# Cross attention with routed experts on one Trainium2 core: value products of two steps in one block, and work moved from VectorE to ScalarE

## The reference, cut to what matters

```python
x = x + xattn(layernorm(x), ctx, mask)     # x, ctx: 8 x 256 x 512, mask: 8 x 1 x 512
x = x + ffn(layernorm(x))
# xattn: q, k, v = W @ input + b, 16 heads of 16 rows
dot  = mask * (q^T k) / 4 - (1 - mask) * 1e6          # 512 x 512 for each batch and head
amap = softmax(dot, axis=-1) * mask
out  = einsum('bhts,bhds->bhdt', amap, v)
# ffn: 2048 tokens of 512, 8 experts, the best two of each token
logits = x @ gate^T ; weights of the best two, divided by their sum
out = sum over the two of  w2_e @ (silu(g) * u),  g, u = split(w1_e @ x)   # w1: 704 x 512, w2: 512 x 352
```

## Time and profile before

| | us |
|---|---|
| median of 3 runs | 869.19 (865.51 to 871.01) |
| the profiled execution | 871.53 |
| its span, first to last instruction | 869.7 |
| PE busy in the span | 801.8 (92%) |
| DVE busy | 553.6 (64%) |
| POOL busy | 370.3 (43%) |
| ACT busy | 318.6 (37%) |
| mean granted clock of TensorE | 0.972 |

### The profile page before, as it was taken

One profiled execution on the slowest core, in us unless ns is written; L12 is line 12 of the kernel. 1 busy time (PEld: TensorE's weight loads), 2 busy tenths in 40 slices (PEclk: granted clock), 3 DMA queues, 4 the chain that ended last, 5 costly groups with the idle time before them and its releaser, 6 DMA issues. The chain is left out here.

```text
span 869.7 us, 13002 instructions
## 1 busy us (share of the span) xinstructions
PE 801.8 (92%) x3757; PEld 365.1 (42%) x3758; DVE 553.6 (64%) x1071; ACT 318.6 (37%) x619; POOL 370.3 (43%) x392
## 2 busy tenths in 40 slices
PE   5888898989999998999989988899999999999993
PEld 2322332333333433433333332365555665665661
DVE  5778887889888887888877874445433333333331
ACT  0035465556565565665655666522000000000000
POOL 7544364556565655655745423334211221211221
PEclk9579999999999999999999999999999999999997
DMA  6745577666766866856845542354648546354332
GB/s 188 231 129 145 172 203 221 200 209 210 231 206 184 264 196 182 257 163 177 244 127 160 172 113 83 94 144 110 152 89 227 133 110 172 65 156 72 72 51 34
DMA packets 84524, 138.02 MB, mean 159 GB/s; under 512 B 14765, under 2 KB 40685, under 8 KB 84474
## 3 DMA queue, kind: packets, MB, share of 16 engines
q1 hardware_dynamic: 68970, 108.65, 41.8%
q0 software_dynamic: 7744, 17.86, 10.7%
q10 hardware_dynamic: 7760, 10.89, 4.5%
HBM read 77.36 MB, written 59.36 MB: 157 GB/s over the span
## 5 line engine op out<-in xcount | busy, mean ns | idle before, releaser
L843 ACT ACTIVATE pr<-sc 128x512 f32<-128x512 f32 x512 | 267.1, 603 | 219.5 <-PE sc L1507 219.3
L990 DVE TENSOR_REDUCE mx<-tile 128x2 f32<-128x1024 f32 x256 | 309.0, 1216 | 55.9 <-PE tile L1519 50.3
L1507 PE MATMUL sc<-qk 100*128 100x512 bf16 x512 | 154.8, 384 | 9.9 <-DMA qk<-mxt 7.2
L1519 PE MATMUL tile<-qk 97*128 97x512 bf16 x496 | 150.9, 388 | 14.0 <-DVE mx L990 7.9
L765 POOL DMA_INDIRECT out_dram<-xin,ids x36 | 56.4, 1566 | 224.0 <-DVE ids L1312 220.0
L1545 PE MATMUL pvb<-pr,vp 128*32 128x512 f32 x1024 | 138.0, 611 | 0.0
L1660 PE MATMUL pvb<-wring,qkf 128*128 (+1 forms) x216 | 98.7, 593 | 1.6 <-DVE qkf L1322 1.6
L720 POOL TENSOR_SCALAR parts<-qkf 128x512 bf16<-128x512 f32 x31 | 46.9, 1512 | 123.3 <-DVE qkf L1074 119.3
L1519 PEld LDWEIGHTS tile<-qk 97*128 97x128 bf16 x496 | 35.0, 98 | 145.6 <-issue 75.7
L1639 PE MATMUL tile<-wring,xh 128*128 x288 | 91.3, 460 | 0.0
L1639 PE MATMUL sc<-wring,xh 128*128 x288 | 91.2, 459 | 0.0
(11 more groups left out here) (158 smaller groups left out, 789.1 us busy)
## 6 DMA issues: line engine op xcount, KB each, us to landing
qk<-stack_d SPq DMA_DIRECT2D x32, 768.0 KB
stack_d<-parts SPq DMA_DIRECT2D x32, 384.0 KB, 3.1
wring<-w_dram SPq DMA_DIRECT2D x32, 352.0 KB, 7.2
cin<-routed_d ACTq DMA_DIRECT2D x36, 257.0 KB, 3.6
stack_d<-parts SPq DMA_DIRECT2D x32, 256.0 KB, 3.1
pv_d<-ov SPq DMA_DIRECT2D x32, 256.0 KB, 3.4
xin<-x_dram SPq DMA_DIRECT2D x16, 256.0 KB, 5.4
cin<-ctxt_dram SPq DMA_DIRECT2D x8, 512.0 KB, 6.3
```

The source lines that it names most:

```text
L843: nc.scalar.activation(pr[s % 2][:, j, :], sc[(32 * u + 4 * s + j) % NSC][:, :], ACT.Exp, scale=SCALE).then_inc(exped.sem, 1)
L990: dve.tensor_reduce(cols, t[:, :, :], X, ALU.max, negate=True).then_inc(drained.sem, 1)
L1507: nc.tensor.matmul(sc[(32 * u + 4 * s + j) % NSC][:, :], ks[half(u)][0:ALL_ROWS, h, c * P:c * P + P], qs[half(u)][0:ALL_ROWS, h, :], start ...
L1519: last = nc.tensor.matmul(t[:, i, :], qs[half(w)][0:RAW_ROWS, h, c * P:c * P + P], ks[half(w)][0:RAW_ROWS, h, :], start=True, stop=True)
```

## The change

Five edits, which hang together:

1. PE's order in units 2 to 15 is written out by hand. The products now stand in blocks of two: those of steps 6 and 7 of the unit before in step 0, those of steps 0 and 1 in step 2, 2 and 3 in step 4, 4 and 5 in step 6. Tiles are placed around them; `count_early` in the last unit moves from step 2 to step 4, `transpose_rows(0, 0)` stays at the end of step 5. DVE's `unit` and the list of tiles (`STEADY`) follow. `product(TAIL, 6)` moves behind the last unit.
2. `pr` gets a third buffer (`NPR = 3`). Its space comes from `mall` and `mrow`, which now lie in `ov`.
3. ACT normalizes the inputs from its third unit on (`normalize` in step 1). POOL makes the shift for it, one small instruction more.
4. ACT copies the second token row (`token_twin` in step 3, and twice in the second part) in place of DVE's second `token_normalize`.
5. DVE reads the logits from PSUM, without the copy `lg`. On POOL `token_rstd` comes before `values_out`.

The first two units keep their order (`front`, `front_events`).

```diff
+NPR = 3
+STEADY = (0, 1, 2, "v", 3, 4, 5, 6, "q", "xT", 7, 8, 9, 10, "logits", 11, 12, "maxT", 13, "k", "ranks", 14, 15)
...
-        pr = [sb(f"pr{i}", [P, 4, T]) for i in range(2)]
+        pr = [sb(f"pr{i}", [P, 4, T]) for i in range(NPR)]
...
+                pool.wait_ge(rstd.sem, rstd.at(u, "pow"))
+                pool.tensor_scalar(at[:, 10:11], at[:, 6:7], at[:, 8:9], -1.0, ALU.mult, ALU.mult
+                                   ).then_inc(rstd.sem, 1)
...
+            def token_twin(u):
+                act.wait_ge(normed2.sem, normed2.at(u, "n"))
+                nc.scalar.activation(xa[:, half(u), 1, 0:T], xa[:, half(u), 0, 0:T], ACT.Copy
+                                     ).then_inc(twin.sem, 1)
...
+                act.wait_ge(rstd.sem, rstd.at(u, "shift"))
...
+                nc.scalar.activation(xh[:, parity(w), half(w), :], xin[:, half(w), :], ACT.Identity,
+                                     bias=at[:, 10:11], scale=at[:, 8:9]).then_inc(normed.sem, 1)
...
-                            if j == 0 and (due := pved.at(u, s, back=2)) is not None:
+                            if j == 0 and (due := pved.at(u, s, back=NPR)) is not None:
...
+                    if s == 1 and u > 1:
+                        normalize(u - 1)
+                    if s == 3 and has(u - 2):
+                        token_twin(u)
...
-                if step == 0:
-                    dve.tensor_copy(lg[:, :], tile_of(u, "logits")[:, 0, 0:E]).then_inc(drained.sem, 1)
...
-                    dve.max(v8[:, :], lg[:, :]).then_inc(choice.sem, 1)
+                    dve.max(v8[:, :], tile_of(u, "logits")[:, 0, 0:E]).then_inc(choice.sem, 1)
```

DVE's `unit` now has the two halves of the reciprocals with the query's drain and the input statistics between them:

```diff
+                maximum(u, *pair_of(u, 5))
+                reciprocals(u, 0)
+
+                maximum(u, *pair_of(u, 6))
+                token_normalize(u)
                 if u == TAIL:
                     plan_early()
...
+                projection_out(u, 0)
+                batch_stats(u, 0)
+                batch_stats(u, 1)
                 reciprocals(u, 1)
-                projection_out(u, 0)
```

More of the change, by code:

```diff
@@ L131, in tile_events @@
         max_ = [(n, ("max", *pair)) for pair in pairs_of(n, s)]
-        ev += max_[:1]
-        if s == 7 and has(n - 2):
-            ev.append((n, "ranks"))
-        ev += max_[1:]
-        ev += [(n, name) for name in fillers(n, s)]
+        ev += max_
+        if s == VALUES_AT[n]:
+            ev.append((n, "v"))
+        if s == 3:
+            ev.append((n, "q"))
         if n == 0 and s == 0:
@@ L141, in tile_events @@
         ev += [(n, ("maxT", *part)) for part in maxima_of(n, s)]
-        if s == 7 and has(n + 3):
+        if s == 7:
             ev.append((n, "k"))
-        if n == TAIL and s == 2:
-            ev.append((n, "early"))
-        if n == LAST - 1 and s == 7:
-            ev.append((n, "count"))
+    return ev
+def tile_events(n):
+    if 0 <= n < len(FRONT):
+        return front_events(n)
+    ahead = {"v": 1, "q": 3, "k": 3, "xT": -2, "logits": -2, "ranks": -2, "maxT": 1}
+    ev = []
+    for name in STEADY:
+        if name == "xT" and n == TAIL:
+            ev.append((n, "early"))
+        if name == "maxT":
+            if has(n + 1):
+                ev.append((n, ("maxT", n + 1, ALL)))
+        elif name in ahead:
+            if has(n + ahead[name]):
+                ev.append((n, name))
+        elif has(pair_of(n, name)[0]):
+            ev.append((n, ("max", *pair_of(n, name))))
+    if n == LAST - 1:
+        ev.append((n, "count"))
     return ev
@@ L369, in attention @@
         rstd2 = Count(sem("rstd2"), of(-2, "eps", "pow"))
-        normed2 = Count(sem("normed2"), of(-2, 0, 1))
-        choice = Count(sem("choice"), of(-2, "v8", "i8", "i8f", "sel", "selb"))
+        normed2 = Count(sem("normed2"), of(-2, "n"))
+        twin = Count(sem("twin"), of(-2, "t"))
+        choice = Count(sem("choice"), of(-2, "v8", "i8f", "sel", "selb"))
         gate_exp = Count(sem("gate_exp"), of(-2, "e"))
@@ L1691, in unit @@
                         project(u, 0)
-                        transpose_tokens(u)
-                    if u == TAIL and s == 2:
-                        count_early()
-                    if s == 4:
-                        logits(u)
-                    if u == TAIL and s == 5:
-                        transpose_rows(0, 0)
                     for w, g in maxima_of(u, s):
@@ L1720, in _ @@
             pe.sem_inc(down_done, 1)
-            for u in range(UNITS):
+            for u in range(len(FRONT)):
+                front(u)
+            for u in range(len(FRONT), UNITS):
                 unit(u)
@@ L1745, in _ @@
             off = gate(0, 0)
+            product(TAIL, 6)
             product(TAIL, 7)
```

210 lines of the change are left out of this document (136 added, 74 removed).

## The result

The changed kernel takes 890.38 us (median of 4 runs, 887.23 to 897.46), the kernel before 868.12 (median of 4, 865.51 to 871.01): a ratio of 1.0267, 95% interval 1.019 to 1.0344. The forecast was 869.0, no change, with 856 to 883 as its range. The time lies above that range. One of the four executions of a0 further down, the 901.51 one, ran in the chip's slower state, so a0 is taken by its other three, 882.77 to 895.71 with a median of 891.17.

What follows compares the result with a forecast made beforehand. PE was taken to bound the kernel, busy 386.7 of 411.5 us in units 2 to 14. The terms -8.6 - 4.1 + 8.4 + 2 + 0 + 3 = +0.7 gave 869.9 against the median, stated as 869, range 856 to 883.

Steps and rivals of the forecast that it cites:

- Some signs of the prediction: Expected in the profile if right: about 31 to 32 us a unit, 3 to 4 us wait before the first rows' transpose.
- Blocks of two: PE, units 2 to 14: four fewer product entries and exits a unit, 0.16 us each, -8.6 us in 13 units.
- Less on DVE: DVE loses about 1.1 us of work a unit; PE's 10.6 us of waits for it shrink by 6.5, taken as -4.1.
- half a hit: POOL's additions stretching DVE's split or choice: 0.5 us a unit, where a full hit was 1.1.
- The third rival: POOL holds DVE's split and choice in each of 13 units, 14.3 us instead of 6.5: 877 us, chance 0.10.
- The reciprocals and the stack: Later reciprocals delay SP's stack DMA; PE waits 0.7 us before raw pair 12 in 12 units: +8.4 us.
- the upper end: Longest landing taken for the stack DMA, 7.5 us from issue to PE's release.
- The denominators: Step 0's later store delays the load of `den`; DVE waits about 1 us in odd units: +2 us.
- the maxima: From transposed maxima to the next unit's first score, as close as before; 4.6 us of waits left unchanged: 0.
- The last unit: Count behind 18 scores at ACT's pace, at +11.3; transpose at +21.4, expert part at +26.6 or later: +3 us.
- ACT at nothing: ACT's two added operations, about 1.1 us of a 31.65 us unit, were costed at nothing.

Runs made afterwards that it cites:

- a0: The changed kernel run again with no edit: 891.17 us (3 runs), ratio 1.0242 to the kernel before.
- b3: Changed kernel, blocks kept, four mends: last unit's count earlier, POOL's residual waiting for the choice, second reciprocals earlier, ACT's row copy two steps later: 859.29 us, ratio 0.9901.
- b2: As b3, but with each block of two products split by one raw pair: 865.50 us, ratio 0.9949.
- b1: Changed kernel with POOL's residual waiting for the choice of experts and all blocks split by a raw pair: 871.61 us, ratio 1.0033.
- a2: Changed kernel with one wait more on POOL, its residual starting only after DVE's selb: 882.71 us, ratio 1.0177.
- f1: Changed kernel with only the fourth block split, raw pair 12 put between products 4 and 5: 889.74 us, ratio 1.0242.
- a3: Changed kernel with all four blocks of two products split by one raw pair each: 884.28 us, ratio 1.0179.
- f2: Changed kernel with the other three blocks split and the fourth kept: 892.36 us, ratio 1.0264.
- c4: b3 without POOL's wait, so the residual goes as soon as it can: 869.76 us, ratio 1.0022.
- b4: The kernel before the change with POOL's residual waiting for DVE's choice of experts: 863.78 us, ratio 0.9930.
- d1: Changed kernel with one mend, the second pair of reciprocals right behind the seventh maximum: 874.06 us, ratio 1.0107.
- c1: b3 with the second pair of reciprocals put back late, where the change has them: 875.75 us, ratio 1.0073.
- a1: Changed kernel with the last unit's count_early moved back to step 2, ahead of products 0 and 1: 889.59 us, ratio 1.0254.
- c3: b3 with the last unit's count put back to step 4: 865.11 us, ratio 0.9965.
- d3: Changed kernel with one mend, ACT's copy of the token row two steps later: 891.27 us, ratio 1.0273.
- c2: b3 with ACT's copy of the token row put back to step 3: 866.94 us, ratio 0.9998.

## Why the prediction was wrong

Some signs of the prediction came as written (31.9 us a unit, a wait of 3.87 before the fetched rows), and the time did not. In the profiled execution units 2 to 14 cost 3.0 more where the sum had 2.3 less, the last unit 8.9 more where it had 3, and 3.4 lie in the front and the expert part, where it had nothing.

**Blocks of two, -8.6: right in sign, once the rest is mended.** (4 x 0.16 is 0.64 and not 0.66, so -8.3.) A block took 1.85 us, and b3 against b2 is -4 to -6. Where the reciprocals are late, the blocks cost: b1 against a2, without POOL's hold, is 11.1 the other way. With the fourth block, raw pair 12 stands ahead of both products, and that is 0.9 us too early for a late mask row. f1 bears out the place (the waits went), not the price: with POOL's hold in the way it gained nothing. Why all four blocks split gave a3 5 to 7 us where f1 and f2 gave none stays open; the intervals of the three overlap.

What such a wait costs the rows show. In a0, PE ahead of and in the block behind a short wait, and the stretch before and in it:

```profile
313.84 0.61 PE L1554 MATMUL tile<-qk 97*128 97x512 bf16 x2 [0.43 <-DMA qk<-mrow_d]
314.37 3.61 PE L1580 MATMUL pvb<-pr,vp 128*32 128x512 f32 x16
```

```profile
305.00:314.00 9.00, 8.20 (x50) 3.36 (x49) 7.78 (x14) 6.81 (x13) 7.43 (x6) 1.00 0.89 262
314.40:317.80 3.40, 3.40 (x17) 0.56 (x16) 1.40 (x2) 0.00 (x0) 1.91 (x2) 0.50 0.75 254
```

The granted clock was 1.00 up to the wait and 0.50, the 1.2 GHz level, for 3.4 us behind it. Not every wait has this behind it: in a0 a wait of 1.52 us ended at 388.57, and the clock was 1.00 for the 5.4 us behind it. The block fell into that stretch, 1.7 us longer than 1.92, and ACT got no scores meanwhile (busy 0.00).

**Less on DVE, -4.1: wrong in sign. This is a failed step.** PE's waits for DVE in units 2 to 14 were to fall; they were 11.1 us (8.1 and 2.5 of the earlier trace rows, and 0.5 before the token rows' transpose) and are 14.1 (10.1 before the ranks, with the 7.2 called "issue", 3.2 for the token row, 0.8 before raw pairs). The work taken away was not too small, 16.9 us where I had 14.3: I took L945's 0.54 for both operations, and `normalize` took 0.73. I had named the mechanism with the earlier trace rows and laid out the new order to see whether POOL's additions would meet `split_maxima`. Then I took half a hit, 0.5 us a unit. L1049 and L1051 together show 18.8 us in 13 units, and 6.4 where POOL waits (a2): 12.4, near 1.0 in each. The third rival's size, 14.3 us, was near; I gave it a chance of 0.10. The hold on the split costs 5.6 to 8.5 us after the change (a2, with overlapping intervals) and 10.5 in company (c4); before the change the hold cost 5 to 6 (b4), on `selb`. So the change made it dearer by 0 to 3 us, in company by about 5, instead of giving back 4.1. No run gives DVE its two operations back, so what the relief alone is worth stays open. b4 shows that the 8.1 us of waits, most of the 10.6 by which I had bounded it, came from the hold and not from a full DVE. The Trainium skill (SBUF — State Buffer, section "SBUF: two separate sides") states that the two engines' shared port is locked for the whole instruction. The trace agrees as far as it goes: L1051 ended 0.15 after POOL's L761.

**The reciprocals and the stack, +8.4: the place was right, and the size was the largest error. This is the other failed step.** The forecast wait of 0.7 us in 12 units came as 3.3 us in the 12 units of the profile shown and 4.8 in a0, so it was even less than forecast, and 7.0 us from issue to release is between the 6.3 I took and the upper end. Yet to move the reciprocals back up gave 12 to 17 us (d1), and to put them late cost 15 to 16.5 (c1). The step that failed is that it took a wait to cost its own length in one place. Late reciprocals did three things: the mask row came late (6.7 us of waits in c1); the clock was at its lower level behind such waits and behind some others (8.0 us more PE busy in c1, 6.9 in a0 against d1; 13.7 us at 0.50 in c1 and in a0, none in b3 and d1); and the residual, which needs them, slid onto the split of the maxima (part of 5.1 us of DVE in a0 against d1). The clock varies between executions: in the profile shown above it was at 0.50 for only 3.4 us of the 12 units. The trace of the kernel before already had a sign for it. SyncE's waits, in the kernel before (124 to 530 us) and after (124 to 535 us):

```profile
SPq L507 <- DVE rec L974: 15.8, 6, 5.8
```

```profile
SPq L520 <- DVE rec L1016: 66.3, 13, 7.8
```

Before, SyncE stood for the reciprocals in 6 of 13 units, 15.8 us; now in all, 66.3 us. Not all of this is delay, since some of its other waits are shorter. What it delays for certain is the stack: issued 1.8 us after the query's first matmul before and in d1, 4.15 after the change.

**The denominators, +2, and the maxima, 0.** Waits for the turned maxima were 4.6 us and are 3.3 in the units. DVE waited 4.0 us for `den` where it had waited 0.8. No run tested this alone; nothing in b3 speaks for more than the +2.

**The last unit, +3: the chain right, the pace wrong.** Measured +8.8 in the profile. The chain from count to transpose was forecast at 10.1 us and took 9.8. But the count came at +14.7 instead of +11.3, since I let ACT set the pace, and PE at 3.6 us a block did; and behind the fetch PE was slow again. The early count gives 0 to 2 back in the changed kernel (a1; its last unit is 2.7 shorter than a0's) and 5.8 in the mended one (c3).

**ACT at nothing: right in the changed kernel (d3), wrong in a mended one (c2, 7.6).** It is hidden only as long as something else is later.

The sum with what was measured in place of the terms: -4 to -6 for blocks (their part in the mask row's lateness is in the reciprocals' term), 0 to +5 for the hold, +12 to +17 for the reciprocals, 0 to +6 for the last unit, and the denominators' +2 as forecast: +8 to +26, against a measured +22.3. That the measured value lies inside proves little, with terms that overlap and a range this wide. The four mends taken out of b3 one at a time sum to 16.5 + 10.5 + 7.6 + 5.8 = 40 us, all four together (a0 against b3) are 30 to 32: part of what each costs is the same time, of which the clock's loss is a likely share.

## What to carry to other kernels

A small operation that is moved within its engine carries all that waits for it: before moving it, read what the DMA queue's own waits say, and list what stands behind the store in that queue. A wait of half a microsecond on PE can cost several times its length, by the granted clock behind it (1.7 us more in the block behind 0.43 us of waiting, though not every wait did this), so a forecast that adds up waits alone can come out low. When a merge seems to lose, mend the waits around it first: here the change with four small moves is about 1% faster than the kernel before, and one wait on POOL alone makes the old kernel 0.7% faster.

## What was not expected of the hardware

After a wait of 0.43 us the granted clock was 0.50 for 3.4 us (a0), and a block of 16 product matmuls took 3.61 us, where it takes 1.92. PE had been busy for 8.2 of the 9.0 us in front. The changed kernel's executions lay at 882.8 to 897.5 us, those of b1, which has no wait for the mask row in the 12 units, at 870.6 to 874.7. That such waits make the spread is not shown: d3, with seven of them, lay within 4.7 us.

A 32x128 cast of 0.21 us and an addition of 0.28 took up to 1.3 us beside POOL's addition of 1.27. POOL loses nothing: with its wait added, its busy time in the 12 units is about the same (213.8 us in a0, 213.0 in a2), and the split beside it is back at its own length because POOL starts later.
